# A message-passing kernel in eight rounds: the low halves of the messages made by POOL instead of DVE in three of them

## What is computed

```python
# SAGE layer, three times
msg = x[src]
mean = segment_sum(msg, dst, n) / maximum(count, 1)[:, None]
return mean @ Wl + bl + x @ Wr
# GCN layer, twice
norm = dinv[row] * ew * dinv[col]
msg = (x @ W)[row] * norm[:, None]
return segment_sum(msg, col, n) + b
```

## Time and profile before

| what | value |
|---|---|
| median of 3 runs | 5308.14 us (5303.43 to 5312.59) |
| the profiled execution | 5311.44 us |
| its span | 5309.5 us |
| mean granted clock of TensorE | 0.948 |
| busy share of the span | PE 82%, DVE 64%, ACT 46%, POOL 37% |

### The profile page before, as it was taken

The page is one execution under the profiler, slowest core; times in us unless marked ns, Lnnn a source line. Parts: engine busy times, 40 slices in busy tenths (PEclk is TensorE's granted clock), DMA queues, the critical chain, the costliest instruction groups (busy, mean ns, idle before and its releaser), DMA issues.

```text
span 5309.5 us, 129104 instructions
## 1 busy us (share of the span) xinstructions
PE 4380.3 (82%) x25128; PEld 2877.8 (54%) x25129; DVE 3373.9 (64%) x10612; ACT 2416.9 (46%) x4973; POOL 1940.3 (37%) x1890
## 2 busy tenths in 40 slices
PE   6998988777778888767777688886899996888896
PEld 4664554444445555445554445443677773676773
DVE  6554444787545555458886788875566664777775
ACT  2443342555257777536664576663122211333332
POOL 5660782764043343026540544400433312333310
PEclk9999999899889999988999899997999998999998
DMA  4663785566234444335553566653444433443332
GB/s 139 217 211 125 245 263 173 188 207 193 89 121 148 152 146 148 114 108 175 175 166 97 175 210 219 214 165 107 139 138 138 138 107 114 125 125 121 111 114 83
DMA packets 443918, 815.60 MB, mean 154 GB/s; under 512 B 70872, under 2 KB 76818, under 8 KB 443828
## 3 DMA queue, kind: packets, MB, share of 16 engines
q1 hardware_dynamic: 389172, 697.28, 38.8%
q0 software_dynamic: 54656, 117.32, 8.9%
HBM read 480.10 MB, written 334.22 MB: 153 GB/s over the span
## 4 chain that ended last, share of the span: by engine, by line
PE 46%; issue 15%; DVE 12%; ACT 8%; DVEq 6%; POOL 5%; DMA 4%; ACTq 3%; SPq 1%; POOLq 0%
PE p_agg L1163 7%; PE p_edge L1150 7%; PE p_agg L1165 7%; PE p_tr L1150 6%; POOL raw L713 4%; PE p_agg L1198 4%; DVE stats L1716 3%; DVE onehot L1613 3%; ACT u L940 2%; ACT o L921 2%; PE p_wide L1285 2%; PE p_agg L1191 2%; PE p_dense L1217 2%; PE p_dense L1219 2%; PE p_dense L1241 2%
## 5 line engine op out<-in xcount | busy, mean ns | idle before, releaser
L1163 PE MATMUL p_agg<-onehot,msg 128*128 128x512 f16 (+1 forms) x2848 | 1129.1, 396 | 523.3 <-issue 211.2
L713 POOL DMA_INDIRECT raw<-node_s,src_i x980 | 972.6, 992 | 1378.2 <-DMA node_s<-o 555.1
L1165 PE MATMUL p_agg<-onehot,msg 128*128 128x512 f16 (+1 forms) x2848 | 1130.0, 397 | 0.0
L1613 DVE TENSOR_SCALAR onehot<-iota,place 128x512 f16<-128x512 f16 x2058 | 699.5, 396 | 367.7 <-PE p_agg L1198 309.4
L1163 PEld LDWEIGHTS p_agg<-onehot,msg 128*128 x2848 | 281.4, 99 | 864.1 <-issue 715.3
L713 POOL DMA_INDIRECT raw<-node_x,src_i x392 | 381.5, 973 | 543.3 <-DMA feature<-more_masked 254.8
L921 ACT ACTIVATE o<-v_ring,nmr,rstd 128x128 f32 (+1 forms) x1176 | 472.8, 482 | 94.6 <-DVE nmr L1732 90.0
L1604 DVE TENSOR_SCALAR onehot<-iota,dst_f,negbase 128x512 f16 (+1 forms) x790 | 314.9, 446 | 278.8 <-PE p_agg L1165 181.3
L1716 DVE BATCH_NORM_STATS2 stats<-v_ring 128x6 f32 (+1 forms) x1960 | 420.4, 279 | 111.3 <-DVE v_ring L1705 55.3
L1198 PE MATMUL p_agg<-h_in,w 128*128 128x512 f32 x784 | 444.3, 650 | 37.9 <-DMA h_in<-feature 36.8
L940 ACT ACTIVATE u<-v_ring,nmr,rstd 128x128 f32 (+1 forms) x784 | 312.5, 481 | 224.2 <-DVE res_in L1762 151.0
(11 more groups left out here) (267 smaller groups left out, 7988.8 us busy)
## 6 DMA issues: line engine op xcount, KB each, us to landing
node_s<-o SPq DMA_DIRECT2D x392, 256.0 KB
h_in<-feature SPq DMA_DIRECT2D x392, 256.0 KB
feature<-u SPq DMA_DIRECT2D x294, 256.0 KB
node_x<-o SPq DMA_DIRECT2D x294, 256.0 KB
res_in<-node_x SPq DMA_DIRECT2D x294, 256.0 KB
h_in<-node_s SPq DMA_DIRECT2D x196, 256.0 KB
h_t<-dinv_scratch SPq DMA_DIRECT2D x196, 256.0 KB
h_in<-in_x SPq DMA_DIRECT2D x98, 256.0 KB
```

The lines of the kernel that those rows point to most:

```text
L713: nc.gpsimd.indirect_dma_start(out=raw[:, (e % RING) * BATCH + j, :], out_offset=None, in_=src_d, in_offset=bass.IndirectOffsetOnAxis(ap=s ...
L1163: nc.tensor.matmul(p_agg[:, a, :], tile_ap(msg, t, 0, D), oh, start=first, stop=True, skip_group_check=True)
L1165: return nc.tensor.matmul(p_agg[:, a, :], tile_ap(msg, t, D, 2 * D), oh, start=False, stop=True, skip_group_check=True)
L1613: last = V.tensor_scalar(tile_ap(onehot, EVERY * a + j), iota[:, :], place[:, bass.ds((it * 2 + a) * EVERY + j, 1)], None, ALU.is_equal)
```

## The change

In the rounds with a `norm` among those that begin early (`lows_by_pool`: the third, fifth and sixth), POOL makes the low halves of batches 1 to 27. Batch 0 stays with DVE. POOL's loop becomes: gather batch e, weigh batch e - 1, make the low half of batch e - 2. DVE's loop over batches goes away in these rounds. PE can no longer rely on the order of DVE's program, so it reads the count of batches from the list and waits for `q.lo_done` ahead of `first_half(it + 1, 0)`.

```diff
--- before.py
+++ after.py
@@ -315,6 +315,8 @@
             sem("first_rows"), sem("first_in"), sem("first_high"), sem("first_low"))
         early = [r for r, rd in enumerate(rounds) if r and rd.kind in (SAGE, GCN)]
 
+        lows_by_pool = [r for r in early if rounds[r].norm]
+
         def split(r):
             return sum(x <= r for x in early)
 
@@ -782,6 +784,14 @@
                         raw[:, 0:EVERY, :], raw[:, 0:EVERY, :],
                         weight[:, 0:EVERY].unsqueeze(2).to_broadcast([P, EVERY, D]), ALU.mult).then_inc(first_in, 1)
 
+                def low(e):
+                    wait(pool, q.hi_done, e + 1)
+                    wait(pool, q.lo_done, e)
+                    nc.gpsimd.tensor_tensor(msg[:, e * BATCH:(e + 1) * BATCH, D:2 * D],
+                                            raw[:, (e % RING) * BATCH:(e % RING + 1) * BATCH, :],
+                                            msg[:, e * BATCH:(e + 1) * BATCH, 0:D], ALU.subtract
+                                            ).then_inc(q.lo_done.semaphore, 1)
+
                 for e in range(BATCHES):
                     if e >= RING:
                         wait(pool, q.copied if rel else q.lo_done, e - RING + 1)
@@ -795,7 +805,12 @@
                         hand_over(e - 1)
                     elif e < 2:
                         hand_over(e)
+                    if e > 2 and r in lows_by_pool:
+                        low(e - 2)
                 hand_over(BATCHES - 1)
+                if r in lows_by_pool:
+                    low(BATCHES - 2)
+                    low(BATCHES - 1)
                 if rel:
                     wait(pool, q.copied, BATCHES)
                     pool.sem_inc(q.copied.semaphore, 1)
@@ -1290,7 +1305,7 @@
 
                 def step(it):
                     if exists(it + 1):
-                        if k == 3:
+                        if k == 3 or r in lows_by_pool:
                             these, (now, after) = odd_list(pe, PT, it * 2 + 1)
                         elif rel:
                             (e0, e1, e2), (now, after) = later_list(pe, PT, it * 2 + 1)
@@ -1321,6 +1336,7 @@
                                 residual_sum(it - 2, a)
                             turn_rows(it - 3, 0)
                         if exists(it + 1):
+                            wait_apart(pe, q.lo_done, these[1])
                             first_half(it + 1, 0, after)
                         layer_rows(it, 1)
                         if k == 5:
@@ -1336,6 +1352,8 @@
                     if exists(it + 1):
                         if rel:
                             wait_apart(pe, q.lo_done, these[0] * 2)
+                        elif r in lows_by_pool:
+                            wait_apart(pe, q.lo_done, these[1])
                         first_half(it + 1, 0, after)
                     if k == 0:
                         second_half(it, 1)
@@ -1661,6 +1679,8 @@
 
                 def list_of(it):
 
+                    if exists(it + 1) and r in lows_by_pool:
+                        return None, pair_list(dve, PT, it * 2 + 1)[0]
                     if exists(it + 1):
                         return odd_list(dve, PT, it * 2 + 1)
                     if exists(it):
@@ -1669,7 +1689,7 @@
 
                 def take_in(these):
 
-                    if these[0]:
+                    if these[0] and r not in lows_by_pool:
                         each_batch(dve, *these[0], batch)
 
                 def further(it, a, these):
@@ -1945,7 +1965,10 @@
                         V.tensor_tensor(msg[:, j0:j1, D:2 * D], raw[:, j0:j1, :], msg[:, j0:j1, 0:D],
                                         ALU.subtract).then_inc(done, 1)
 
-                early_batches(dve, PT, batch, first_batch if r in early else None)
+                if r in lows_by_pool:
+                    first_batch()
+                else:
+                    early_batches(dve, PT, batch, first_batch if r in early else None)
                 more_onehots(0, 0, single_list(dve, PT, 0))
                 if k >= 4:
                     scaled_sums(0, 0)
```

## The result

The change takes 5327.15 us (median of 8 runs, 5318.35 to 5338.4) against 5308.5 for the kernel before (8 runs, 5296.01 to 5314.81). The ratio is 1.0038 with a 95% interval of 1.0029 to 1.0047: slower by 0.4%, some 19 us. The forecast was 5332.

The account below looks back on a forecast made before the run. No engine was full; a ring of waits between engines was taken to set the pace. Starts +16 and even parts 0, +8 and 0 gave +24 us on the profiled 5311.4, or 5332 on the median's scale, range 5262 to 5385.

Parts of the forecast that it names:

- The hold: Even parts: POOL's weighing and low, 3.4 us in one piece, stop DVE where it has one-hots and normalization to do.
- The price of a low: On POOL: each of 81 subtractions of 128x896 takes 1.70 us, like the weighing; the skill's cycle count gave 1.94.
- The starts: Start of third, fifth and sixth rounds: PE waits for batch 1's low; +5, +8 and +3 us remain, range 0 to +25.
- The third round's even part: Third round, once the pace is even: a cycle of three pairs stays at 27.4 us, a change of 0.
- The fifth round: Fifth round's even part: a cycle of three pairs goes from 32.6 to 33.3 us, +8 us over 11 cycles.
- ACT's own work covers about 1: Fifth round: of 1.7 + 2.15 us a cycle that POOL holds DVE, about 1 is hidden behind ACT's work.
- The sixth round: Sixth round's even part: a cycle of three pairs stays at 41.0 us, a change of 0.
- PE's part: On PE: an added wait and three register instructions a pair, set against DVE's removed loop, cost 0, within 5 us.
- 16 + 0 + 8 + 0: Forecast sum in us: late round starts, then even parts of the third, fifth and sixth rounds; +24 in all.
- Rival B: Faster: POOL's lows fall where DVE waits or isn't held; 5247 us with full floors, 5286 with half; chance 0.34.
- its floor of 24.8: Third round: shortest cycle of three pairs without collisions, set by POOL needing 12.4 us a batch; 2.6 under 27.4.
- The floors of the fifth and sixth: Even parts of these rounds: a cycle of three pairs without collisions takes about 30.5 and 38.7 us.

Follow-up runs that it names:

- e4: The change with POOL's low subtracting only the first of a batch's seven tiles, order and waits kept: 5226.8 us, the kernel before 5305.3.
- e2: The change with batch 1's low half made earlier on POOL, right behind the gathers of batch 2: 5304.7 us, the kernel before 5305.3.
- e5: The kernel before with only PE's part of the change, DVE still making every low half: 5323.1 us, ratio 1.0024.
- e11: The change with POOL's lows placed for each round, plus some 256 PE instructions before the first relational round, 207 counts jumped over: 5273.4 us, ratio 0.9938.
- e6: The change with batch 1's low early and, in the fifth round only, the later lows between POOL's gathers: 5291.2 us, ratio 0.9959.

## Why the prediction was right, and where it wasn't

The total was right, 5332 for 5327, and so was the sign. Two of its terms are right by mechanism, and the others miss in ways that nearly cancel: that the total came so near is luck.

- **The hold.** That the low on POOL stops DVE, and that low and weighing in one piece fall on the normalization, is what the trace shows (3.99 for an `nmr` of 0.17) and e4 confirms. The Trainium skill, "SBUF — State Buffer", section "Who interferes with whom", calls the pair of ports that the two engines share an exclusive lock. The trace agrees, and a DVE instruction whose recorded start lies 0.4 us ahead of POOL's was held too.
- **The price of a low.** "I take 1.70, since operation, size and number of inputs are the weighing's": it is 1.89. The 1.94 estimated from the Trainium skill's "GPSIMD Engine Reference", section "Elementwise — side-by-side cycle accounting", is nearer, and the weighing's row was not the better guide.
- **The starts.** PE's waits were forecast as 14.2, 13.0 and 9.0, and are 14.9, 14.2 and 9.2. But "+5, +8 and +3" kept to the end is 8.5, 7.7 and 8.0 by e2: 24, at the end of the range of 25, not 16. Less came back than I took.
- **The third round's even part.** "I take 27.4: 0" is the step that failed most: 25.4, a gain of 2.0 a cycle, 24 us over the round by e2. The hold was there as priced, 24.8 us in 18 pairs (`nmr` 22.9 and one-hots 1.9) for lows of 24.5 that left. What I had too small is what left beside them. I took the loop alone, at "some 0.25 us a pair", but with DVE's busy time unchanged its idle time in the window fell from 32.4 to 21.1 (length less busy), 0.63 a pair. The traces show two halves of it. The idle time right behind the loop's instructions, ahead of L1599 (2.8) and `deg` at L1693 (2.9), is gone: 0.32 a pair, near what I took. The other half I put at nothing: the idle time ahead of `stats` (L1716, now L1736) fell from 15.6 to 9.9, and what it lost stood behind DVE's reading of the list (10.4 there before, 4.3 after), which takes less time now (DVE's sequencer, source view in the windows, before and after, min/median/max in ns):

```profile
L384 DVEq TENSOR_LOAD <-lists x18: 1002/1360/1574, 1089.9 to 1245.5; - x18
...
L386 DVEq TENSOR_LOAD <-lists x18: 741/744/758, 1086.4 to 1231.2; - x18
```

Three words are read in both; why it took longer before is not shown, and no run took loop or reading away alone. The lows that left were dearer too: 24.5 us over six cycles are 4.1 a cycle, where I took the round's mean, 3.64.

- **The fifth round.** Forecast 33.3 a cycle, measured 34.1, so +19.5 us by e2 where I took +8. "ACT's own work covers about 1" was too kind: ACT's wait for L1782 grew by 17.8 us over 18 pairs, nearly all that the products were held more (19.4), so that some 0.3 a cycle was covered.
- **The sixth round.** Forecast 41.0, measured 40.6: the one-hots are held by 16.9 us in the window for the 13.1 of the lows, as foreseen, and DVE's idle time fell by 6.4, which outweighs the difference. 13.4 us won by e2, where I took 0; 7.7 of them come in the last eight pairs, when all batches are there, an end for which I took 0 too. No run shows why.
- **PE's part.** "0, within 5 either way" is the step that failed by omission: the waits cost nothing (e5's rounds: +0.3, -1.4, 0.0), but 44 more instructions cost some 12 us in a round that the change doesn't touch, in two branches of PE that take 8.0 and 4.8 us for at most 0.33. I counted what the added instructions take where they run and not what they move.

So 16 + 0 + 8 + 0 stands against 24 - 24 + 20 - 13 + 13, which is 20 and the medians' 19. Rival B was partly true: the third round came down to 25.4, near its floor of 24.8, the sixth only from 41.0 to 40.6, with a floor of 38.7, and e11 shows that the idea of the change was good for 0.6% with the lows in the right places and PE's instructions moved on. The floors of the fifth and sixth were priced well, as e4 has 31.3 and 38.0; its 23.5 in the third lies under the floor, which was reckoned from POOL's time for a batch with a full low.

## What to carry to other kernels

When work goes to POOL to relieve DVE, don't count the microseconds that DVE loses; ask which of DVE's instructions will be waiting while POOL works, and who waits for that one. The same 1.9 us cost the fifth round 20 us (e2) or nothing (e6), by where they stood among POOL's gathers. And look at the unedited rounds of the trace too: a longer program of one engine can cost there what the edit won.

## What the runs showed of the hardware

- An instruction of DVE on 8 elements per partition is held as well as one on 1024: `nmr` 3.99 for 0.17, through two POOL instructions in a row, and a product 2.70 for 1.19. Cutting POOL's instruction in three made its work longer (2.33 for 1.90), and the held lines took about as much.
- Near the start of the first relational round PE's branch at the head of the loop over batches takes 0.08 to 0.33 us or 4.2 to 8.0, by where PE's instructions lie: none of the long ones in before, two after 44 more instructions, none again after some 256. The Trainium skill, "Runtime: NRT & Kernel Launch", section "Instruction fetch mechanics", says that instructions come in blocks of 16 KiB, 256 instructions each, and that a branch out of the blocks at hand waits for a fetch. The runs agree with the packets of 16 KB, with the 256 and with the branch. After such a pause PE also begins at the lower clock: from 3773.40 to 3776.00 of the change, right behind 7.75 us of idle, the granted clock is 0.50, the lower of its two levels (1.2 and 2.4 GHz), and matmuls of one form take 0.61 to 0.63 there and 0.38 ahead of the pause.
- A count of a semaphore takes 0.15 us on PE even where nobody waits for it (212 of them 32 us); jumping over 207 of them cost nothing that the trace shows: PE's first multiplication behind them begins as in before, after 18.1 us of idle where it was 18.0.
